# Carrying token number and weight with the experts' rows, and scattering finished rows into the output

## The reference, cut to what matters

```python
gates = _sinkhorn(gate_logits)              # 8 rounds of normalising, (tokens, experts)
vals, idx = jax.lax.top_k(g_t, m)           # each expert picks its m = n // 8 best tokens
routed = take_along_axis(xn, idx)           # the rows that the experts picked
outputs = einsum('ebhmi,ehio->ebhmo', routed, expert_w) * gate_values
routed_back = zeros.at[idx].set(outputs)    # a token picked by several experts keeps the last
x = x + routed_back
```

## Time and profile before

| what | us |
|---|---|
| median of three runs (lowest to highest) | 3428.75 (3427.73 to 3429.03) |
| the profiled execution's own time | 3419.65 |
| its span, first to last instruction | 3417.8 |
| MLP's last logits to the sink stage's first DVE instruction | 3184 to 3202.2 |
| sink stage to the first scatter | 3202.2 to 3294.1 |
| scatter to `expert_in` | 3294.1 to 3316.2 |
| expert stage | 3316.2 to 3384.1 |
| return | 3384.1 to 3417.8 |

### The profile page before, as it was taken

One profiled execution on the slowest core, in us unless ns is written; L12 is line 12 of the kernel. 1 busy time (PEld: TensorE's weight loads), 2 busy tenths in 40 slices (PEclk: granted clock), 3 DMA queues, 4 the chain that ended last, 5 costly groups with the idle time before them and its releaser, 6 DMA issues.

```text
span 3417.8 us, 46446 instructions
## 1 busy us (share of the span) xinstructions
PE 3069.5 (90%) x16511; PEld 1753.2 (51%) x16511; DVE 1705.4 (50%) x3897; ACT 1034.2 (30%) x2211; POOL 1489.2 (44%) x1477
## 2 busy tenths in 40 slices
PE   6999999888999799699999896999899999999436
PEld 4543466576676444367777663444433333444222
DVE  6623355487344332566677633432277777322532
ACT  2212422396222222234344331220144444321100
POOL 0477777587755266323222104632166655000011
PEclk9999999999999899889999998999999999999658
DMA  4320012201111334234343444210276666200015
GB/s 162 129 72 7 7 53 73 90 20 22 44 49 46 107 138 177 85 109 116 105 119 108 126 136 160 82 43 1 62 239 198 190 197 175 67 25 11 15 65 173
DMA packets 250439, 324.79 MB, mean 95 GB/s; under 512 B 131455, under 2 KB 161025, under 8 KB 250212
## 3 DMA queue, kind: packets, MB, share of 16 engines
q1 hardware_dynamic: 186052, 178.30, 16.7%
q0 software_dynamic: 52736, 138.06, 13.1%
q10 hardware_dynamic: 11424, 5.47, 0.6%
HBM read 216.75 MB, written 105.65 MB: 94 GB/s over the span
## 4 chain that ended last, share of the span: by engine, by line
PE 77%; DVE 11%; issue 4%; ACT 3%; DMA 2%; POOL 1%; SPq 1%; ACTq 0%; POOLq 0%; DVEq 0%
PE bank L2492 7%; PE bank L1429 5%; PE bank L2484 4%; PE bank L672 3%; PE bank L488 3%; PE bank L1209 3%; PE bank L2199 3%; PE bank L2627 3%; PE bank L2620 3%; PE bank L1050 3%; DVE delta_tmp L2005 2%; PE bank L693 2%; PE bank L2181 2%; PE bank L724 2%; DVE delta_Us L2008 2%
## 5 line engine op out<-in xcount | busy, mean ns | idle before, releaser
L2461 POOL DMA_INDIRECT conv_src<-xn_rows,conv_rec x288 | 272.2, 945 | 305.0 <-DMA conv_rec<-sorted_edge 128.3
L455 POOL DMA_INDIRECT sorted_bias<-perf_rec,place x256 | 260.3, 1017 | 160.3 <-issue 83.1
L2492 PE MATMUL bank<-conv_msg,conv_hot 128*128 128x512 f32 x576 | 273.1, 597 | 1.8 <-ACT conv_msg L2509 1.8
L1800 POOL TENSOR_TENSOR delta_dec<-delta_dec,delta_gt 128x512 f32<-128x512 f32 x64 | 67.6, 1057 | 388.4 <-ACT delta_dec L1842 388.4
L2528 DVE TENSOR_TENSOR conv_msg<-bank,conv_src 128x512 f32<-128x512 f32 x288 | 185.5, 686 | 46.9 <-PE bank L2484 40.5
L2509 ACT ACTIVATE conv_msg<-conv_msg 128x1024 f32<-128x1024 f32 x144 | 152.2, 1057 | 102.6 <-DVE conv_msg L2528 102.6
L1050 PE MATMUL bank<-bias_prod,bias_hot 128*128 128x256 f32 x640 | 148.0, 387 | 29.1 <-issue 12.9
L2484 PE MATMUL bank<-conv_we,conv_eT 64*128 64x512 f32 x576 | 165.2, 650 | 1.5 <-ACT conv_eT L2506 1.5
L1034 POOL TENSOR_TENSOR bias_prod<-bias_col,bias_rec 128x512 f32<-128x512 f32 x128 | 147.4, 1180 | 19.0 <-PE bank L1050 18.6
L1050 PEld LDWEIGHTS bank<-bias_prod,bias_hot 128*128 128x128 f32 x640 | 120.8, 193 | 56.7 <-issue 32.9
L656 POOL DMA_INDIRECT sorted_edge<-rec,place x128 | 127.4, 995 | 38.4 <-issue 36.8
(11 more groups left out here) (476 smaller groups left out, 6614.6 us busy)
## 6 DMA issues: line engine op xcount, KB each, us to landing
delta_qk<-slot_qkv SPq DMA_DIRECT2D x32, 512.0 KB, 3.8
delta_kv<-slot_qkv SPq DMA_DIRECT2D x32, 512.0 KB, 3.8
sorted_edge<-sort_pad SPq DMA_DIRECT2D x8, 1440.0 KB, 7.5
conv_rec<-sorted_edge SPq DMA_DIRECT2D x18, 640.0 KB, 5.9
slot_out<-delta_o SPq DMA_DIRECT2D x64, 128.0 KB, 1.7
conv_src<-xn_rows,conv_rec POOLq DMA_INDIRECT x288, 3.7
X<-in_x SPq DMA_DIRECT2D x4, 1024.0 KB, 10.5
sorted_bias<-perf_rec,place POOLq DMA_INDIRECT x256
```

The costliest lines, as they stand in the source:

```text
L455: POOL.indirect_dma_start(out=sorted_bias, out_offset=bass.IndirectOffsetOnAxis(ap=place[:, 0, c:c + 1], axis=0), in_=rec0[:, c, :], in_of ...
L2461: POOL.indirect_dma_start(out=src[:, n % 4, j, :], out_offset=None, in_=xn_rows, in_offset=bass.IndirectOffsetOnAxis(ap=rec[:, g % 3, k + ...
L2492: a = PE.matmul(bank[n % 2][:, :], hot[:, g % 2, k + j, :], msg[:, q, j, :], start=j == 0, stop=j == 1)
```

## The change

Each row of `expert_in` becomes 16 floats longer (`RW = D + 16`). Column 512 holds N minus the token's number, column 513 its weight; an empty slot is all zero, so its number reads as N, which is out of bounds. The tokens are copied as they stand before the experts to a new HBM array `tokens` and into `out` itself, as soon as each group of `X` is final. In the expert stage DVE reads the numbers of a tile (`find`), POOL gathers these tokens from `tokens` into `xg` (`bring`), DVE forms product times weight plus token in one instruction, and POOL scatters the result into `out` by the same numbers. `expert_out`, its stores, and the whole return stage are gone. The sink stage's eight tables move from an allocation of their own into free space of `h1`.

```diff
+RW = D + 16
+    parts["number"] = N - np.arange(NT)[None, :] * P - np.arange(P)[:, None]
-        expert_in = scratch("expert_in", (N, D))
-        expert_out = scratch("expert_out", (N, D))
+        expert_in = scratch("expert_in", (N, RW))
+        tokens = scratch("tokens", (N, D))
...
         def sync():
             for x in range(FE):
                 weights(x)
+            for i in range(NB):
+                SP.wait_ge(*ended.at(NB * (KC - 1) + i + 1))
+                for to, sign in ((tokens, x_kept), (out, x_out)):
+                    SP.dma_start(to[4 * i * P:4 * (i + 1) * P, :].rearrange("(t p) d -> p t d", p=P),
+                                 X[:, 4 * i:4 * i + 4, :]).then_inc(*sign.up(16))
...
-                step(DVE.tensor_reduce(slot_w[:, :], V["tmp"].rearrange("p e t -> p t e"), AX.X, ALU.add))
+                step(DVE.tensor_reduce(xn[:, :, D + 1], V["tmp"].rearrange("p e t -> p t e"), AX.X, ALU.add))
+                DVE.tensor_copy(xn[:, :, D], const("number"))
...
-                step(DVE.tensor_copy(slot_of[:, :], r16[:, :]))
...
         def sync():
-            for t in range(NT + 4):
-                if t < NT:
-                    if t >= 4:
-                        SP.wait_ge(*turned.at(t - 3))
-                    SP.dma_start(xe[:, t % 4, :], expert_in[t * P:(t + 1) * P, :]).then_inc(*xe_in[t % 4].up(16))
+            for t in range(NT):
                 if t >= 4:
-                    u = t - 4
-                    SP.wait_ge(*ye_ready.at(u + 1))
-                    SP.dma_start(expert_out[u * P:(u + 1) * P, :], ye[:, u % 4, :]).then_inc(*ye_out[u % 4].up(16))
+                    SP.wait_ge(*turned.at(t - 3))
+                    SP.wait_ge(*ye_ready.at(t - 3))
+                SP.dma_start(xe[:, t % 4, :], expert_in[t * P:(t + 1) * P, :]).then_inc(*xe_in[t % 4].up(16))
+
+        def pool():
+            POOL.memset(xg, 0.0).then_inc(*cleared.up())
+            POOL.wait_ge(*cleared.at(1))
+            POOL.wait_ge(*x_kept.now())
+            POOL.wait_ge(*x_out.now())
+            def bring(t):
+                POOL.wait_ge(*numbered.at(t + 1))
+                if t >= 4:
+                    POOL.wait_ge(*ye_ready.at(t - 3))
+                POOL.indirect_dma_start(
+                    out=xg[:, t % 4, :], out_offset=None, in_=tokens,
+                    in_offset=bass.IndirectOffsetOnAxis(ap=number[:, t:t + 1], axis=0), bounds_check=N - 1,
+                    oob_is_err=False).then_inc(*xg_in[t % 4].up(16))
+            bring(0)
+            bring(1)
+            for t in range(NT):
+                if t + 2 < NT:
+                    bring(t + 2)
+                POOL.wait_ge(*ye_ready.at(t + 1))
+                POOL.indirect_dma_start(
+                    out=out, out_offset=bass.IndirectOffsetOnAxis(ap=number[:, t:t + 1], axis=0), in_=ye[:, t % 4, :],
+                    in_offset=None, bounds_check=N - 1, oob_is_err=False).then_inc(*ye_out[t % 4].up(16))
...
         def vector():
+            def find(t):
+                DVE.wait_ge(*xe_in[t % 4].at(16 * (t // 4 + 1)))
+                DVE.tensor_scalar(number[:, t:t + 1], xe[:, t % 4, D:D + 1], -1.0, float(N), ALU.mult, ALU.add).then_inc(*numbered.up())
+            for t in range(3):
+                find(t)
             for t in range(NT):
                 DVE.wait_ge(*product.at(t + 1))
+                DVE.wait_ge(*xg_in[t % 4].at(16 * (t // 4 + 1)))
...
-                DVE.tensor_copy(ye[:, t % 4, :], bank[4 + t % 4]).then_inc(*ye_ready.up())
+                DVE.scalar_tensor_tensor(ye[:, t % 4, :], bank[4 + t % 4], xe[:, t % 4, D + 1:D + 2], xg[:, t % 4, :], ALU.mult,
+                                         ALU.add).then_inc(*ye_ready.up())
+                if t + 3 < NT:
+                    find(t + 3)
...
-        rows_in = sig.several(NT, "sw")
-        ended = sig.take()
-        x_out = sig.take("hw")
-        for t in range(NT):
-            POOL.indirect_dma_start(
-                out=xn[:, t, :], out_offset=None, in_=expert_out,
-                in_offset=bass.IndirectOffsetOnAxis(ap=slot_of[:, t:t + 1], axis=0)).then_inc(*rows_in[t].up(16))
-            DVE.wait_ge(*rows_in[t].at(16))
-            DVE.scalar_tensor_tensor(X[:, t, :], xn[:, t, :], slot_w[:, t:t + 1], X[:, t, :], ALU.mult,
-                                     ALU.add).then_inc(*ended.up())
-            SP.wait_ge(*ended.at(t + 1))
-            SP.dma_start(out[t * P:(t + 1) * P, :], X[:, t, :]).then_inc(*x_out.up(16))
```

32 lines of the change are left out of this document (18 added, 14 removed).

## The result

| | kernel before | changed kernel |
|---|---|---|
| median of six runs each | 3428.24 us (3416.36 to 3439.67) | 3393.76 us (3388.74 to 3401.92) |
| profiled execution: own time, span | 3419.65, 3417.8 us | 3401.92, 3400.1 us |
| granted clock over the span | 0.950 | 0.950 |

The ratio is 0.9909, with a 95% interval of 0.9891 to 0.9926: 31 us less, 25 to 37. Forecast were 28.9 us less and 3399.9 us, in a range of 3396 to 3409. So the forecast saving lies inside the interval, and by the ratio the time is 0.9909 x 3428.75 = 3397.5 us, inside the range, while the median itself came out 6 us under the forecast and 2 us under the range.

What follows compares the result with a forecast made beforehand. PE was taken to bound the expert stage, with nothing running beside the final return. Return removed -33.7, chain left +4.5, added ahead +0.3 give -28.9 us: 3428.75 becomes 3399.9 us, range 3396 to 3409.

Steps and rivals of the forecast that it cites:

- The stretch behind the last product: End of program: 33.7 us of return replaced by four links (DVE, POOL start, scatter landing, end) of 4.5 us, saving 29.2.
- The nearest row: Last scatter's landing: taken as 2.72 us from the last scatter to expert_in, same queue and row count, HBM target.
- The far end: Last scatter's landing: upper case of 6.5 us, from a gather under the return's heavy traffic.
- When the last product ends: Sign at the end of the expert stage: the last product ends within 1 us of 3384.4.
- What is added ahead: Before the expert stage: a small DVE copy, 0.17 us at most, and a longer first load, together 0.3 us.
- The stores: Before and into the sink stage: eight 1 MB stores, 51 us at 163 GB/s, cost 0; stores-or-landing rival's chance 0.05.
- The loads: Expert stage: the load of tile t + 4 now waits for ye of tile t, with slack 2.3 us at least.
- less the 0.44 of a turn: Expert-stage loads: 0.44 us for a turn, subtracted from the 7.74 us between the product of t and turning t + 4.
- POOL: no bound: Expert stage: POOL's round takes 3.15 us, under PE's 3.87; rival of POOL as bound +2 to +8.6 us, chance 0.08.
- The low-clock rival: Expert stage: late loads make PE pause and stay at 1.2 GHz, 15 tiles at 3.87 us, +58, so 3458; chance 0.04.
- 7.5 such tiles: Expert stage: number of low-clock tiles, at 3.87 us each, from which the 28.9 us saving changes sign.
- Traffic: Expert stage: 0.71 MB per tile in 3.87 us, 184 GB/s against 119 before; the sign was 170 to 190.

Runs made afterwards that it cites:

- e1: The changed kernel again, no edit: 3394.89 us, ratio 0.9909 to the kernel before.
- e3: The changed kernel with its eight 1 MB stores from X moved into the sink stage: 3398.79 us, ratio 0.9920 to the kernel before.
- e5: The changed kernel with each expert-stage load that waits for ye issued two tiles later: 3464.04 us, ratio 1.0100 to the kernel before.
- e6: The changed kernel with each expert-stage load that waits for ye issued one tile later: 3388.38 us, ratio 0.9880 to the kernel before.
- e9: e8 plus one unused matmul behind each of PE's 39 sums in the sink stage: 3393.02 us, ratio 0.9905 to the kernel before.
- e11: The e9 kernel timed in more rounds, on one chip with e12: 3765.94 us, ratio 0.9901 to the kernel before.
- e12: The changed kernel, unedited, timed in more rounds on one chip with e11: 3768.89 us, ratio 0.9914 to the kernel before.
- e4: The changed kernel with each gather of tokens issued twice, so three POOL transfers per tile: 3400.93 us, ratio 0.9916 to the kernel before.
- e8: The changed kernel with nine unused PE matmuls after the first ten scatters, before the expert stage: 3398.23 us, ratio 0.9901 to the kernel before.
- e2: The kernel before with only the eight early stores added, into arrays nobody reads: 3427.00 us, ratio 1.0000 to the kernel before.
- e7: The kernel before with only the wider expert_in rows and fill and two unread DVE copies: 3427.54 us, ratio 0.9991 to the kernel before.

## Why the prediction was right

**The stretch behind the last product: right.** Forecast -29.2 us, measured 33.68 to 4.40, -29.28; in e1, e3, e5, e6, e9, e11 and e12 it is 4.31 to 4.40, in e4 and e8 4.73 and 4.80. Link by link, DVE took 0.76 (0.75), POOL's restart 0.79 (0.92, taken from the earlier trace rows), landing and end 2.85 (2.82). The nearest row of the right queue and direction was the right choice for the landing. The far end, 6.5 us under the return's traffic, belonged to another traffic.

**When the last product ends: off by 11 us.** The sign was "within 1 us of 3384.4", and it ended at 3395.7. A time counted from the start of the program was a bad sign, since 10.0 us of this are the late start of this execution and 1.5 its way to the sink stage. From the sink stage on the parts came as forecast.

**What is added ahead: +0.3 forecast.** The sink stage is 0.1 us longer in the first profile and no longer in e1 (90.7), the landing 0.03 us, the expert stage 0.10 us. From the start of the sink stage to the end before had 215.58 us and the changed kernel 186.38 and 185.98 (e1), so 29.2 and 29.6 us less, for 28.9 forecast.

**The total: 31 us by ratio against 28.9.** The interval of 25 to 37 holds the forecast, and the stretches give 29.2 to 29.6. What is left, some 2 us by ratio and 5 by medians, no run of mine explains. The three timings of the changed kernel give 34.5, 34.6 and 35.4 us by medians and 31, 31 and 33 by ratio, all more than the stretches, so it need not be scatter; but each interval holds 29.3. e2 and e7, with parts of the change that the profile prices at nothing, came out 2.5 and 1.9 us under the kernel before by medians, and by ratio at 1.0000 and 0.9991, inside their intervals. What the new memory layout does ahead of the last stages was not tested by itself. That the forecast of the median was 6 us too high has the same open cause, as the kernel before measured 3428.24 for the 3428.75 that I started from.

**The stores: cost right, term mis-sized.** I had bounded them by the 163 GB/s of the early fill and had them under way for 51 us. Three windows of the changed kernel, and the answer on the line of the stores, say:

```profile
3172.00:3182.00 10.00, 4.83 (x22) 3.93 (x23) 9.83 (x26) 2.14 (x4) 2.33 (x2) 0.51 1.03 400
3182.20:3190.00 7.80, 6.30 (x20) 2.94 (x19) 7.70 (x24) 2.50 (x5) 1.32 (x1) 0.55 1.04 393
3190.00:3196.00 6.00, 5.28 (x27) 2.49 (x26) 3.60 (x8) 2.63 (x5) 1.32 (x1) 1.00 0.99 371
...
DMA to landing us min/median/max: 5.5/7.4/9.3
```

The first is issued at 3172.6 and by 3196 all are done, at 371 to 400 GB/s (the first window still has the end of a load of weights in it) and in less than half the time I gave them. The early fill was no good measure. It did not have the DMA engines to itself, as this window out of its time shows (kernel before), and the packets in it are 0.6 KB in the mean where those of the stores are 2 KB:

```profile
170.00:180.00 10.00, 10.00 (x43) 5.97 (x42) 0.00 (x0) 2.74 (x8) 7.56 (x9) 1.00 0.97 281
```

So 4.2 MB over 25.7 us was a share of the engines, and no rate of theirs. Which part other transfers had and which the packets, no run separates. With the stores the DMA engines are idle before the sink stage begins, where I had them busy in its first 30 us.

**The loads: outcome right, working wrong.** PE never waited before a turn. But the step "less the 0.44 of a turn" failed: tile t + 4 is turned at the end of the 7.74 us. With the changed kernel's landings (line of the loads), 2.5 to 4.5 us and 3.0 in the median,

```profile
DMA to landing us min/median/max: 2.5/3.0/4.5
```

the least slack is 7.74 - 0.75 - 0.1 - 4.5 = 2.4 us and the usual one 3.9. That 2.3 was forecast is luck: the 0.44 taken off in error stood in for a landing that came at 4.5 instead of 4.1. And e6 showed that one tile less leaves almost none and still costs only 0.76 us.

**POOL: no bound, as forecast.** POOL in the changed kernel's timeline:

```profile
3374.48 1.01 POOL L2937 DMA_INDIRECT out<-mlp_h,mlp_number  x1 [1.53 <-DVE mlp_number L2976]
3375.80 1.02 POOL L2926 DMA_INDIRECT mlp_h<-tokens,mlp_number  x1 [0.30 <-issue]
...
3384.80 1.01 POOL L2937 DMA_INDIRECT out<-mlp_h,mlp_number  x1 [4.11 <-issue]
3386.12 1.02 POOL L2926 DMA_INDIRECT mlp_h<-tokens,mlp_number  x1 [0.31 <-issue]
```

A scatter and a gather every 3.87 us, 0.30 between them, and 1.53 us idle before the next pair. 0.30 of that it would need between two issues anyway, so 1.2 us are room. The release named is DVE's number, though POOL waits for `ye`: what came last by the profile need not be what is waited for. At 3384.80 one scatter started 2.6 us late (idle for 4.11 instead of 1.53 us, and nothing that the profile shows ended it). The next ones followed at 0.30 us, so the delay was made up within two rounds, as the forecast argued against this rival. It is no chance: the same transfer, POOL's 26th of the stage, stands behind 4.1 us in e1, e3 and e12 too, and behind 3.8 us in e8, e9 and e11; in e4 the 26th had 1.48. So it hangs on a place in POOL's program, but which of its properties does it stays open. e4 showed the far side: even at 3.97 us per round the stage does not move. A transfer costs POOL 1.02 us here, not 0.94, and the restart 0.79 instead of 0.95, which makes a round 3.13 us where the forecast had 3.15.

The Trainium skill ("SBUF — State Buffer", SBUF: two separate sides) has POOL held up only while DVE holds the lock: in a two-port mode, or with two inputs in SBUF against a POOL operation that reads SBUF. The prediction left this condition out. The new DVE instruction takes its product from PSUM and only one tile from SBUF, so the second case does not apply, and whether the first does no run shows. Nothing is held in the trace: with DVE's 0.76 us in every tile, e4's round of 3.97 us is three times 1.02 and 0.30 us and nothing else. No run varies the DVE instruction.

**The low-clock rival: did not come, and its price was put on the wrong cause.** The clock was 1.00 in the stage. e5 shows that late loads would have been enough for a slower kernel (1.0100), mostly from the pauses themselves, 45.9 us, and only for 10.2 us from a clock that fell in every second tile. So the price of 3.87 us per tile, and with it the point of "7.5 such tiles", does not stand: each late tile cost 4.7 us in the mean, and with all twelve late the sign turns at about 2.4 us each.

**Traffic.** 165 GB/s in the stage, for 184 worked out and 170 to 190 given. The bytes per tile were right, the count was not: in the 57.7 us of the window fall 15 scatters, but only 13 gathers (POOL's 28 less the scatters) and the 12 loads that wait for a product, the first four having gone ahead. 12 x 0.27 + 13 x 0.22 + 15 x 0.22 MB over 57.7 us are 163 GB/s.

## What to carry to other kernels

When a stretch at the end runs on engines that stand idle in the stage ahead (here POOL, while PE bounds that stage), cost the move in two sums: what stays behind the last product, taken from the nearest row of the same queue and direction, and the round of the engine that takes the work on, against the bound's pace. In a stage as short as this such a round may even be 0.1 us over the pace, as in e4, because the head start absorbs it; but a load that comes later than its room costs its full lateness in every tile, as in e5, so the waits of the loads want a closer look than the busy times. And compare two profiled executions from a common event on: here their totals differed by 17.7 us where the stretch that was changed differed by 29.3.

## What was not expected of the hardware

- Stores of 1 MB from SBUF moved at 393 GB/s while nothing else did (3182.2 to 3190), where the early fill landed at 163 beside other transfers.
- PE came through pauses of 3.5 us in each tile with an average clock of 0.90, but not evenly: every second tile took 5.30 instead of 3.60 us for its eight products (e5). In the sink stage the clock went from 0.51 to 0.87 with one idle matmul of 128x512 behind every sum (e1, e9).
- One and the same program came to its last part at 3167.2 and at 3173.2, and its variants between 3156.2 and 3176.9. In the pair of before and after the 10 us arose between 434 and 681 us, with the granted clock at 0.97 and 0.82 in the first part of it. A clock below 1.00 can also be a consequence: on the chip of e11 and e12, 375 us slower, PE stood idle behind ACT, which waited up to 44.6 us for something outside the profile.
- POOL takes an issue every 1.3 us without a pause, beside a busy PE and a DMA share of 0.71, and has a hold of 2.6 us at one and the same place of its program in most profiles.
